# A linear-attention layer on one Trainium2 core: the next batch's transposes issued ahead of the token sums instead of behind them

## What is computed

```
xn  = layernorm(x)
Q, K, V = split(xn @ W_in.T + b_in)
Q, K = rope(Q), rope(K)                  # first 128 of 256 features
A = sum over tokens of (K / |K|) * V     # one row of 256 per batch
x = x + (A * Q) @ W_out.T + b_out
```

## Time and profile before

| | |
|---|---|
| median of 3 runs | 572.07 us (571.98 to 572.12) |
| the profiled execution | 571.89 us, of which span 570.1 us |
| PE busy | 560.8 us (98%), PEld 530.7 us (93%) |
| DVE, ACT, POOL busy | 464.7 us (82%), 370.6 us (65%), 210.9 us (37%) |
| granted clock of PE | 1.00 over the span |
| the linear layer's steps 2 to 7 on PE | from 447.1 to 495.8 us of the span |

### The profile page before, as it was taken

The page is one execution under the profiler, slowest core; times in us unless marked ns, Lnnn a source line. Parts: engine busy times, 40 slices in busy tenths (PEclk is TensorE's granted clock), DMA queues, the critical chain, the costliest instruction groups (busy, mean ns, idle before and its releaser), DMA issues.

```text
span 570.1 us, 12874 instructions
## 1 busy us (share of the span) xinstructions
PE 560.8 (98%) x4138; PEld 530.7 (93%) x4138; DVE 464.7 (82%) x1475; ACT 370.6 (65%) x1037; POOL 210.9 (37%) x316
## 2 busy tenths in 40 slices
PE   9999999999999999999999999999999999999996
PEld 8899999999999999999999999999999899888885
DVE  4888789778977897798789778977877899878876
ACT  5987556566755766666657555756986677754543
POOL 3782224233223332242234223323347577413221
PEclk9999999999999999999999999999999999999999
DMA  8807000000000000000000000000000000001002
GB/s 325 303 1 231 2 1 3 1 1 0 0 0 0 0 0 0 0 0 0 0 0 0 0 0 0 0 0 1 2 1 1 1 2 1 1 1 38 6 32 77
DMA packets 9152, 14.71 MB, mean 26 GB/s; under 512 B 1568, under 2 KB 6688, under 8 KB 9120
## 3 DMA queue, kind: packets, MB, share of 16 engines
q1 hardware_dynamic: 8848, 14.04, 7.0%
q10 hardware_dynamic: 272, 0.26, 0.1%
HBM read 12.20 MB, written 2.10 MB: 25 GB/s over the span
## 4 chain that ended last, share of the span: by engine, by line
PE 90%; DVE 5%; ACT 3%; DMA 1%; issue 1%; POOL 0%; SPq 0%; DVEq 0%
PE bank L651 71%; PE bank L754 5%; PE bank L736 3%; PE bank L757 2%; PE bank L661 2%; PE bank L943 2%; PE bank L931 2%; PE bank L868 1%; PE bank L738 1%; DMA raw<-in_wk 1%; ACT prob L1157 1%; ACT big L1130 0%; DVE prob L1572 0%; DVE qT L1518 0%; PE bank L679 0%
## 5 line engine op out<-in xcount | busy, mean ns | idle before, releaser
L522 POOL TENSOR_SCALAR prob<-prob,rowinv 128x256 f32<-128x256 f32 (+1 forms) x127 | 96.5, 771 | 267.0 <-DVE rowinv L1588 267.0
L651 PE MATMUL bank<-xT,big 128*128 128x256 f32 x984 | 129.5, 283 | 0.1
L651 PEld LDWEIGHTS bank<-xT,big 128*128 128x128 f32 x984 | 123.2, 191 | 1.0 <-issue 0.2
L1157 ACT ACTIVATE prob<-prob,negmax 128x128 f32<-128x128 f32 (+1 forms) x256 | 112.8, 445 | 8.4 <-DVE negmax L1572 8.4
L651 PE MATMUL bank<-wp,oT 128*128 128x256 f32 x768 | 102.6, 283 | 0.0
L651 PEld LDWEIGHTS bank<-wp,oT 128*128 128x128 f32 x768 | 96.9, 190 | 0.6
L1119 ACT ACTIVATE qT<-bank 128x512 fp32r<-128x512 f32 x68 | 40.6, 597 | 71.5 <-PE bank L651 71.3
L651 PE MATMUL bank<-pT,v 128*128 128x512 f32 (+1 forms) x384 | 79.8, 343 | 0.6 <-DVE pT L1518 0.4
L651 PEld LDWEIGHTS bank<-pT,v 128*128 128x128 f32 x384 | 63.2, 189 | 9.8 <-issue 0.9
L1518 DVE TENSOR_TENSOR pT<-bank,pT 128x512 fp32r<-128x512 f32 (+1 forms) x128 | 65.2, 551 | 3.0 <-ACT pT L1119 2.9
L1119 ACT ACTIVATE pT<-bank 128x512 fp32r<-128x512 f32 (+1 forms) x128 | 55.2, 484 | 13.1 <-PE bank L754 11.0
(11 more groups left out here) (191 smaller groups left out, 992.4 us busy)
## 6 DMA issues: line engine op xcount, KB each, us to landing
raw<-in_wq SPq DMA_DIRECT2D x4, 512.0 KB, 6.9
raw<-in_wp SPq DMA_DIRECT2D x4, 512.0 KB, 7.3
x<-in_x SPq DMA_DIRECT2D x7, 256.0 KB, 7.0
out<-x SPq DMA_DIRECT2D x6, 256.0 KB, 2.1
raw<-in_w_gu SPq DMA_DIRECT2D x2, 640.0 KB, 5.1
raw<-in_w_in SPq DMA_DIRECT2D x1, 768.0 KB, 4.7
raw<-in_w_down SPq DMA_DIRECT2D x1, 640.0 KB, 6.9
raw<-in_wk SPq DMA_DIRECT2D x1, 512.0 KB, 4.3
```

Source lines behind the costliest of these rows:

```text
L522: m = pool.tensor_scalar(prob[:, j % 2, 0, a:b], prob[:, j % 2, 0, a:b], rowinv[:, j % 2, r:r + 1], None, ALU.mult)
L651: m = pe.matmul(out, lhs(a), rhs(b), start=first and i == 0, stop=last and i == len(passes) - 1, skip_group_check=True)
L1157: m = act.activation(prob[:, j % 2, i, a:b], prob[:, j % 2, i, a:b], ACT.Exp, scale=-1.0, bias=negmax[:, 2 * i + r:2 * i + r + 1], accum_o ...
```

## The change

In step n of PE's `linear` the transposes of batch n + 1 (in step 7: of the gated layer's batch 0) stand ahead of the token sums of batch n - 1, not behind them. Steps 2 to 7 are affected. No instruction is added, removed or resized; the other engines' programs are as they were, and so are all waits.

```diff
@@ linear(n), engine PE
                 if n > 1:
                     linear_k(n, 0)
                     linear_k(n, 1)
+                linear_transpose(n + 1) if n + 1 < NB else gated_transpose(0)
+                if n > 1:
                     linear_sum(n - 1)
-                linear_transpose(n + 1) if n + 1 < NB else gated_transpose(0)
                 if n > 1:
                     linear_out(n - 2)
```

## The result

The change made the kernel slower. In the same session the kernel before took 572.03 us (median of 6, 571.39 to 572.61) and the changed one 574.50 us (median of 6, 574.39 to 574.82): a ratio of 1.0046, 95% interval 1.0036 to 1.0056, which is 2.1 to 3.2 us on 572.07. Forecast was 574.9 us, that is 2.8 us more; the medians differ by 2.47 us. A second session gave 574.57 us against 572.13, ratio 1.0048 (1.0035 to 1.0062).

A forecast was written before the change was run, and what follows sets the result against it. PE, busy 98% of the span, was taken as the bound; waits of 0.46 + 0.93 + 0.43 + 0.98 = 2.8 us on the 572.07 us median gave 574.9 us, range 573.2 to 576.3.

The forecast's parts named there:

- step 2: Linear layer: PE waits 1.55 us for DVE's apply(3), 1.09 us regained before batch 3's keys; 0.46 us left.
- step 3: Linear layer: transposes wait for apply(4), slow beside POOL's `ternary_bias(7)`; PE's lag rises by 0.93 us.
- 4 and 5: Linear layer: PE's lag of 1.39 us covers the wait for DVE's apply; terms 0 and 0.
- step 6: Linear layer: PE waits for apply(7), which comes later as DVE lags by about 1.34 us; term 0.43 us.
- 7, the sums uncovered: Last linear step: PE waits for `gated_apply(0)` with the sums now behind the wait; 1.74 us lost.
- 7, paid back by the gap: Last linear step: the 0.76 us gap before `gated_transpose(1)` closes, leaving 0.98 us of the 1.74 us.
- a full lock between POOL and DVE: At apply(4): it would start after POOL's add and end at 458.97, 0.27 us later, for 3.1 us in all.
- the contention: Rival: apply(4) and POOL's add come apart, so less slow: 1.9 us more, 574.0 us; chance 0.11.
- the tighter loop: Rival: DVE's lag returns to PE through the apply in linear steps 4, 5 and 6: 4.2 us, 576.3 us; chance 0.12.
- absorbed: Rival: DVE, not PE, sets the pace, all 2.8 us of waiting falls into gaps: 572.1 us; chance 0.05.
- Faster: Rival: earlier transposes bring the keys sooner and both PE gaps close: 1.7 us won, 570.4 us; chance 0.03.
- The clock: Rival: PE drops to half rate behind one stall, costing 3.4 us: 578.3 us; chance 0.05.

The follow-up runs named there:

- Step 7 alone: Kernel before with the transposes ahead of the sums in the last of the linear steps only: 572.52 us, ratio 1.0013 (1.0004 to 1.0022).

## Why the prediction was right

Point by point, from the keys of batch 2 (447.09 us before, 446.70 after), the lag of PE:

| step | forecast term | measured term | how measured (before, after) |
|---|---|---|---|
| 2 | 0.46 | 0.33 | keys of batch 3: 8.50, 8.83 |
| 3 | 0.93 | 1.10 | output product: 12.46, 13.89 |
| 4 and 5 | 0 | -0.08 | keys of batch 6: 30.26, 31.61 |
| 6 | 0.43 | 0.46 | output product: 33.87, 35.68 |
| 7, the sums uncovered | 1.74 | 1.74 | output product: 40.69, 44.24 |
| 7, paid back by the gap | -0.76 | -0.93 | `gated_transpose(1)`: 45.00, 47.62 |

Forecast 2.8 us, measured 2.62 at the last row and 2.60 at the gated layer. The mechanism, the place of each wait and the two gaps that close were as written. Four things fell short:

- The payback of step 7 was mis-sized. In step 2 I counted the gap from where the transposes really end, 0.16 us ahead of the row's modelled end; in step 7 I took the row's 0.76 us as it stood. The q products ahead of that gap have the same modelled tail. Step 7 alone shows 0.93 us.
- Step 2's term was too high because its gap, too, held more than I took: from the ternary layer's transposes to the keys of batch 3 it was 1.53 us (454.06 to 455.59) and is 0.36 (455.17 to 455.53), so 1.17 us was paid back and not 1.09, and PE came to it 1.50 us late and not 1.55. The wait itself was right: the row reads 1.39 us, counted from a modelled end, but the keys give way 1.54 us after they start (as from 455.59 to 457.13), at 448.24, and the transposes start at 449.78, so that PE lost 1.54 us; I had 1.55. In the same way step 3's 1.17 us is 1.29. In steps 6 and 7, where keys give way after 1.44 us (as from 484.12 to 485.56), 0.23 is 0.39 and 1.57 is 1.72; I had 0.43 and 1.74.
- In step 3 the transposes started 0.05 us after the apply's end (456.61 + 1.70 = 458.31, then 458.36), as taken. In the kernel before PE also stood some 0.25 us ahead of that step's output product, which no row shows as idle: it starts 0.69 us after the transposes there, and 0.44 in step 5. The term counts it, since it was taken from the start of that product. The term came out higher because step 2's came out lower: together 1.43 us, forecast 1.39. This is no luck, as DVE's apply and not PE sets that time, whatever step 2 cost.
- The prediction took a full lock between POOL and DVE to put the whole 0.74 us of the apply behind POOL's add, and held the row's 458.70 against it. The lock holds one of the two instructions, and the row fits it: the first ended 0.15 us after the add. The sum went by the row, so nothing in it changes.

The rivals: the contention was real and worth 1 us, but neither instruction moved, so it stayed as argued. The lag grew no further than in step 6, so the tighter loop fell. Nothing was absorbed beyond the two gaps, though both paid back more than was taken. Faster fell for the reason given: ACT's queue held the high half, and only with ACT and DVE reordered too did the keys come sooner. The clock did not fall: the granted clock is 1.00 (2.4 GHz) in every stretch from 446.7 to 498 us, through waits of up to 1.57 us in the row, all four right ahead of transposes. That PE-mode transposes don't count as PE being busy the way matmuls do, as the prediction cites from the Trainium skill ("TensorE: Matmul & The Clock Gate", section on the PE-mode transpose), no run here shows.

## What to carry to other kernels

On an engine that runs in order, a piece of independent work ahead of a wait is its cover: before moving a producer forward, look when its own input is ready, and count the wait it will meet less whatever later gap the lag closes. Moving one engine's instruction forward wins nothing while the next engine's queue takes the result at the same place; the early transposes paid only with ACT and DVE reordered, and even then little, by the rows as cover for another wait. A slow instruction that nobody waits for (here an apply stretched by POOL's add) becomes a cost the day its cover is moved.

## What the runs showed of the hardware

Two things that I had not expected, with their numbers. An idle time on PE holds 0.12 to 0.24 us more than its row says when the work ahead of it ends in modelled matmuls: 0.93 us in the row and 1.17 paid back, 0.76 and 0.93, and the four waits of the changed kernel 0.12 to 0.16 more each.

And POOL and DVE held each other up by whole instructions, whichever was under way first. The pair of `tensor_scalar` on DVE took 0.72 us without a POOL add beside it, 1.70 where one was under way, and 2.27 where two ran back to back; each held instruction ended 0.15 us after the one on POOL (457.83 to 457.98 in step 3, 479.61 to 479.76 in step 6). The other way round, POOL's 128x512 add took 1.28 us beside DVE's q products, and 2.00 in the changed kernel, where DVE's L1875 was under way when it started (455.66 to 456.69); the add ended 1.14 us after that instruction, and 1.13 in the kernel before (457.10 to 458.23). So in step 3 DVE's own L1875 held the add, and the add then held DVE's apply. Not every instruction on POOL does this: beside the small `ternary_rstd` (L450, 0.83 us) apply(3) took 0.74 us.
